# Norms one group ahead and a free bank: one change in two phases of a fused two-layer decoder

## The chip, the cores and the metric

The kernel runs on one core of one Trainium2 chip. It is one program that holds a whole two-layer decoder for 16 sequences of 128 tokens with 256 features, written by hand with explicit semaphores. The metric is the device time of the execution in microseconds (us), lower is better. Below, TensorE is the matmul engine (PE in the profile), VectorE is DVE, ScalarE is ACT, GpSimd is POOL and SyncE is SP.

## What is computed

Six blocks follow each other on a residual stream `x` of shape (16, 128, 256); each reads a layer norm of `x`:

```
x = x + attention0(layernorm(x))
x = x + retention(layernorm(x), ctx)        <- the change is here
x = x + spline_ffn(layernorm(x))
x = x + window_attention(layernorm(x))
x = x + cross_attention(layernorm(x), ctx)
x = x + moe(layernorm(x))                   <- and at the start of this one
```

Retention, with two heads of 128, `Wh` per head, and a sum over the batch inside the scores:

```
Q, K, V = xn @ Wh, ctx @ Wh, ctx @ Wh            (per head)
A       = max(|sum_batch(Q K^T / sqrt(128) * decay)|, 1)
O       = A @ V
Y       = (O - mean(O)) / sqrt(var(O) + 0.001) * gn_gamma + gn_beta
W       = relu(xn @ wg_w)
out     = (W * Y) @ wo_w
```

The last block, a mixture of 16 experts with 8 chosen per token and one shared expert:

```
shared  = ((x @ sw1.T) * relu(x @ swg.T)^2) @ sw2.T
xl      = x @ Wdown.T                                  (64 features)
p       = sigmoid(x @ Wg.T), top 8 of p + biases, scaled to a sum of 2.5
out     = shared + (sum_e p_e * expert_e(xl)) @ Wup.T
```

## The kernel before

Each block is a phase with its own queues, one list of instructions per engine, written in `phase_retention` (L717 to L1059) and `phase_moe` (L2127 to L2544). All order is that of the code; an instruction that waits on a semaphore holds up everything behind it on its engine. The eight PSUM banks are `bank[0]` to `bank[7]`. Float32 products that need precision are made by `matmul3` (L31 to L37), three products of a rounded part (`hi`) and a rest (`lo`); ScalarE writes `hi`, and VectorE the difference `lo`.

**Retention, first half.** The 16 sequences are four groups (`GROUP = 4`, `NG = 4`). For group g, VectorE's `normalise(g)` (L858) writes the four normalised sequences to `xn`, which has room for one group. TensorE's `transpose_x(g)` (L973) transposes them into `XB` (banks 0 and 1, one per half of the features). ScalarE's `round_xT(g)` (L813) and VectorE's `split_xT(g)` (L880) make `xT_hi` and `xT_lo` of it, each in one instruction of 1024 columns. TensorE's order for a group is `project_T(g)`, `transpose_x(g + 1)`, `project_gate(2g)`, `score(g)`, `project_gate(2g + 1)` (L1043 to L1049). `project_gate(p)` makes the gate of a pair of sequences in one of two banks (`GATE`), and VectorE's `take_gate(p)` (L888) turns it into `gain` and `shift`. VectorE's loop (L931 to L951) runs `normalise(g + 1)`, `take_gate(2g)`, `split_xT(g + 1)`, in group 0 then `add_out_bias()` (bias and statistics of the last four sequences, whose attention output comes late), `take_gate(2g + 1)`, and in group 0 `finish_stats` and `split_w(1)`. The norm of group 3 needs those statistics and a `pow` on GpSimd (L800).

**Retention, second half.** `mix(p)` (L1009) makes the retention output of a pair of sequences, eight pairs in all, ScalarE copies it to `O`, VectorE takes its statistics in two parts, the first four sequences (`FIRST2`) and the other twelve (`REST2`), each followed by seven small steps (`finish_stats`) and a `pow` on GpSimd (L803). Then `scale(p)` (L899) normalises and gates pair p into `xn`, in slots 0 and 1 for every pair, and so waits for the transposes of the pair before. TensorE does `transpose_wy(p)` (L1015) and then `project_out(p - 1)` (L1024); VectorE's loop (L961 to L969) is `scale(p + 1)`, `split_wyT(p)`, `restat(p - 1)`. SyncE loads the weights of all later phases in this phase (L794).

**Last phase, its start.** `project_latent(g)` (L2457) writes the latent projection of group g to `LAT_BANKS[g % 3]` (banks 2, 3, 4), `mix_latent(g)` (L2357) on VectorE makes `XL` from it. VectorE works these in between the steps of the expert choice (L2393 to L2413). `up_shared(s)` (L2461) makes the gate product of shared step s in `UG` (banks 0 and 1) and the up product in `U1[s % 3]` (banks 2, 3, 4); bank 2 is that of latent groups 0 and 3. `gate_hidden(s)` (L2361) multiplies them. Banks 6, 7 and 5 (`Y`) take the experts' down products, much later. Behind shared step 2, TensorE transposes the chosen gates (L2528 to L2531).

Of the kernel before, what the change touches and what calls it, by code (L numbers as in the profile page):

```python
# [6 lines left out]
F32 = mybir.dt.float32  # L7
F32R = mybir.dt.float32r
BF16 = mybir.dt.bfloat16
ACT = mybir.ActivationFunctionType  # L10
AX = mybir.AxisListType

B, S, D = 16, 128, 256
# [10 lines left out]
def wait(eng, sem, value):  # L24

    if isinstance(value, int) and value <= 0:
        return
    eng.wait_ge(sem, value)
# [688 lines left out]
def phase_retention(nc, a, sem, sb_, bank, X, ident, mean, var_eps, rstd, minus_half, stats, ln_tmp, banks, ret_in, out_bias, ret_loaded, ahead, ahead_loaded, kept, free_attn0, V):  # L717

    local = ExitStack()
    with local:  # L720
# [34 lines left out]
        xT_hi_ready = sem("ret_xT_hi_ready")  # L755
        xT_lo_ready = sem("ret_xT_lo_ready")
        T_done = sem("ret_T_done")
        TT_ready = sem("ret_TT_ready")
# [30 lines left out]
        with nc.Block() as block:  # L789
# [19 lines left out]
            def _(act):  # L809
# [3 lines left out]
                def round_xT(g):  # L813
                    act.wait_ge(x_transposed, g + 1)
                    wait(act, gate_made, 2 * (g - 1))
                    nc.scalar.activation(xT_hi[:, g % 2], XB, ACT.Copy).then_inc(xT_hi_ready, 1)

# [37 lines left out]
            def _(dve):  # L855
# [24 lines left out]
                def split_xT(g):  # L880
                    dve.wait_ge(xT_hi_ready, g + 1)
                    TT_(xT_lo[:, g % 2], XB, xT_hi[:, g % 2].bitcast(F32), ALU.subtract).then_inc(xT_lo_ready, 1)

# [15 lines left out]
                def scale(p):  # L899
                    dve.wait_ge(rstd2_ready, 1 if 2 * p + 1 < GROUP else 2)  # L900
                    wait(dve, wy_transposed, p)
                    for b in (2 * p, 2 * p + 1):
                        STT(O[:, b, :], O[:, b, :], mean[:, b:b + 1], gain[:, b, :], ALU.subtract, ALU.mult).then_inc(scaled, 1)
                    for b in (2 * p, 2 * p + 1):
                        dve.wait_ge(scaled, b + 1)
                        STT(xn[:, b % 2, :], O[:, b, :], rstd[:, b:b + 1], shift[:, b, :], ALU.mult, ALU.add).then_inc(wy_ready, 1)

# [21 lines left out]
                split_w(0)  # L929
                dve.wait_ge(gn_loaded, 32)  # L930
                for g in range(NG):  # L931
                    if g + 1 < NG:
                        normalise(g + 1)
                    take_gate(2 * g)
                    if g + 1 < NG:
                        split_xT(g + 1)
                    if g == 0:
                        add_out_bias()
# [16 lines left out]
                n = finish_stats(nc, dve, stat2, GROUP, stats[:, FIRST2, :], mean[:, FIRST2], var_eps[:, FIRST2], ln_tmp[:, :, FIRST2], 1e-3)  # L955
                group_stats(REST2)
                dve.wait_ge(stat2, n + B - GROUP)
                n = finish_stats(nc, dve, stat2, n + B - GROUP, stats[:, REST2, :], mean[:, REST2], var_eps[:, REST2], ln_tmp[:, :, REST2], 1e-3)
                scale(0)
                dve.wait_ge(stat2, n)  # L960
                for p in range(PAIRS + 1):  # L961
                    if p + 1 < PAIRS:
                        scale(p + 1)
                    if p < PAIRS:
                        split_wyT(p)
                    if p > 0:
                        restat(p - 1)
                    if p == EARLY // 2:
                        next_norms()  # L969

            @block.tensor
            def _(pe):
# [8 lines left out]
                def project_T(g):  # L981
                    pe.wait_ge(xT_lo_ready, g + 1)
                    wait(pe, TT_ready, g)
                    for h in range(H_):
                        ins = matmul3(nc, TB[:, h, :], (G_hi[:, h, :], G_lo[:, h, :]), (xT_hi[:, g % 2, h, :], xT_lo[:, g % 2, h, :]), first=True, last=True)
                    ins.then_inc(T_done, 1)
# [28 lines left out]
                def transpose_wy(p):  # L1015
                    pe.wait_ge(wy_ready, 2 * p + 2)
                    wait(pe, wyT_lo_ready, p - 1)
                    for k in range(KD):
                        for j in range(2):
                            at = (2 * k + j) * 128  # L1020
                            ins = nc.tensor.transpose(WYB[p % 2][:, at:at + 128], xn[:, j, k * 128:(k + 1) * 128], ident[:])
                    ins.then_inc(wy_transposed, 1)
# [1104 lines left out]
def phase_moe(nc, a, sem, sb_, bank, X, ident, mean, var_eps, rstd, minus_half, stats, ln_tmp, w, out, spare):  # L2127

    local = ExitStack()
    with local:  # L2130
# [80 lines left out]

        UG, U1, Y = bank[0:2], bank[2:5], (bank[6], bank[7], bank[5])
        XT_BANKS, LOGITS, LAT_BANKS = (bank[6:8], bank[0:2]), bank[5], bank[2:5]
        LAST_ORDER = (0, 2, 1, 3, 4, 6, 5, 7)
# [3 lines left out]
        with nc.Block() as block:  # L2218
# [105 lines left out]
            def _(dve):  # L2324
# [36 lines left out]
                def gate_hidden(s):  # L2361
# [4 lines left out]
                    else:  # L2366
                        wait(dve, downs_done, (s - NG - 6) // 2 + 1)
                        dst = hidden[:, s % 6, :]
                    TT(dst, U1[s % 3], squared[:, s % 2, :], ALU.mult).then_inc(hidden_done, 1)  # L2369

# [60 lines left out]
            def _(pe):  # L2431
# [29 lines left out]
                def up_shared(s):  # L2461
                    wait(pe, relu_done, s - 1)
                    project(UG[s % 2], 2, s).then_inc(gate_ups_done, 1)
                    wait(pe, XL_ready, (4, 2, 3, 0)[s])
                    wait(pe, hidden_done, s - 2)
                    project(U1[s % 3], 1, s).then_inc(ups_done, 1)

# [200 lines left out]
```

## Time and profile before

| | us |
|---|---|
| three runs | 1082.79, 1083.32, 1086.08 (median 1083.32) |
| the profiled execution, its own time | 1082.19 |
| its span | 1080.4 |
| TensorE busy | 1006.8 (93% of the span) |
| VectorE busy | 779.2 (72%) |
| ScalarE busy | 710.5 (66%) |
| GpSimd busy | 303.5 (28%) |

Retention runs from about 541 to 625 us of the span, the last phase from 927 us to the end. The mean granted clock of TensorE over the span is 0.968 of its full 2.4 GHz. The page's line of DMA traffic, 40 slices of 27 us, has 142 GB/s in the slice from 540 to 567 us (the weights of the later phases) and 1 to 2 GB/s in the twelve after it. In a timeline, each row has the start in us from the span's start, the time in us, the engine, the source line and operation, what is written and read, and in brackets the idle time before it and what ended it. `x8` says that eight like instructions are merged in the row.

### The profile page before, as it was taken

The page shows a single profiled execution, that of the slowest core. Times are in us where ns is not written, and L with a number is a line of the kernel's source. Part 1 is how long each engine was busy: PE and PEld are TensorE (multiplying, and loading weights), DVE is VectorE, ACT ScalarE, POOL GpSimd, SP SyncE. Part 2 cuts the span into 40 slices and gives each one's busy share as a digit, 9 for nine tenths or more (in the row PEclk, how much of TensorE's full clock was granted, in tenths as well). Part 3 has the DMA queues.
Part 4 walks back from the last instruction along what each step waited for, and adds up shares of the span by engine and source line. Part 5 has one row for each costly group of instructions (what it writes and reads, how often), then busy time and mean ns, then how long its engine had stood idle before and what let it go on. Part 6 is the DMA issues. An engine that isn't in the chain of part 4 may idle for free. (4 is left out here: it accounts for less than half of the span.)

```text
span 1080.4 us, 19089 instructions
## 1 busy us (share of the span) xinstructions
PE 1006.8 (93%) x6751; PEld 836.2 (77%) x6751; DVE 779.2 (72%) x1540; ACT 710.5 (66%) x1960; POOL 303.5 (28%) x250
## 2 busy tenths in 40 slices
PE   7999999999999999999978877899998799789998
PEld 3888889889889889888967656677776699565555
DVE  5888867667676677766667788899887344567775
ACT  5888776777777876776722356678787244448882
POOL 1343323323323333233200020244444000102442
PEclk9999999999999999999989888899999799899999
DMA  7221000000000010001050000000000000025432
GB/s 214 81 69 49 2 1 2 1 1 1 1 1 2 1 35 1 1 2 55 24 142 1 1 1 1 1 2 2 2 2 2 2 1 2 15 52 129 103 98 79
DMA packets 31837, 31.79 MB, mean 29 GB/s; under 512 B 8192, under 2 KB 23296, under 8 KB 31744
## 3 DMA queue, kind: packets, MB, share of 16 engines
q1 hardware_dynamic: 31744, 30.59, 10.3%
q8 instruction: 54, 0.88, 0.3%
q14 instruction: 39, 0.32, 0.1%
HBM read 28.35 MB, written 2.23 MB: 28 GB/s over the span
## 5 line engine op out<-in xcount | busy, mean ns | idle before, releaser
L345 POOL TENSOR_TENSOR roped_q<-roped_q,sin_q 128x512 f32<-128x512 f32 x64 | 82.0, 1281 | 301.2 <-DVE sin_q L490 301.2
L1604 ACT ACTIVATE win_P<-banks,win_neg_max 128x128 f32<-128x128 f32 x256 | 91.3, 379 | 27.4 <-DVE win_neg_max L1678 26.9
L345 POOL TENSOR_TENSOR roped_k<-roped_k,sin_k 128x512 f32<-128x512 f32 x64 | 83.3, 1301 | 46.0 <-DVE sin_k L490 46.0
L399 ACT ACTIVATE P<-banks,neg_max 128x128 f32<-128x128 f32 x256 | 90.5, 372 | 5.9 <-DVE neg_max L515 5.6
L433 ACT ACTIVATE oT_hi<-banks,bv_col 128x512 fp32r<-128x512 f32 x64 | 44.1, 689 | 74.2 <-PE banks L663 74.2
L1560 POOL TENSOR_TENSOR win_P<-win_P,win_inv 128x512 f32<-128x512 f32 x64 | 66.9, 1046 | 72.9 <-DVE win_inv L1683 72.9
L408 ACT ACTIVATE sin_k<-banks 64x512 f32<-64x512 f32 x128 | 76.0, 594 | 11.0 <-PE banks L37 9.5
L518 DVE SCALAR_TENSOR_TENSOR oT_lo<-banks,bv_col,oT_hi 128x512 fp32r<-128x512 f32 x64 | 47.9, 749 | 42.5 <-ACT oT_hi L433 42.0
L408 ACT ACTIVATE sin_q<-banks 64x512 f32<-64x512 f32 x128 | 76.0, 594 | 2.9 <-PE banks L37 0.7
L625 PE MATMUL banks<-WO_lo,oT_hi 128*128 128x256 f32 x256 | 72.9, 285 | 0.0
L625 PE MATMUL banks<-WO_hi,oT_hi 128*128 128x256 f32 x256 | 71.6, 280 | 0.0
L625 PE MATMUL banks<-WO_hi,oT_lo 128*128 128x256 f32 x256 | 71.5, 279 | 0.0
L489 DVE SCALAR_TENSOR_TENSOR roped_k<-banks,qk_bias,cos 128x512 f32<-128x512 f32 x64 | 48.0, 750 | 32.6 <-ACT sin_k L408 32.6
L638 PEld LDWEIGHTS banks<-roped_k,roped_q 128*128 128x128 f32 x512 | 67.2, 192 | 2.4
L663 PE MATMUL banks<-PT,V 128*128 128x128 f32 x512 | 68.3, 276 | 0.4 <-ACT PT L420 0.4
L638 PE MATMUL banks<-roped_k,roped_q 128*128 128x128 f32 x512 | 67.5, 275 | 0.0
L2260 POOL TENSOR_TENSOR ret_V<-ret_V 128x512 f32<-128x512 f32 x30 | 38.7, 1292 | 98.9 <-DVE ret_V L2383 98.9
L663 PEld LDWEIGHTS banks<-PT,V 128*128 128x128 f32 x512 | 62.3, 192 | 1.0 <-ACT PT L420 0.9
L2369 DVE TENSOR_TENSOR moe_hidden<-banks,moe_squared 128x512 f32<-128x512 f32 x64 | 44.1, 689 | 25.6 <-PE banks L2477 20.3
L420 ACT ACTIVATE PT<-banks 128x512 f32<-128x512 f32 x64 | 38.2, 598 | 35.4 <-PE banks L615 34.5
L489 DVE SCALAR_TENSOR_TENSOR roped_q<-banks,qk_bias,cos 128x512 f32<-128x512 f32 x64 | 48.0, 750 | 16.3 <-ACT sin_q L408 16.1
L2284 ACT ACTIVATE moe_relu<-banks 128x512 f32<-128x512 f32 x68 | 40.1, 590 | 25.5 <-PE banks L2477 15.7
(403 smaller groups left out, 3218.4 us busy)
## 6 DMA issues: line engine op xcount, KB each, us to landing
moe_gate_of<-moe_gate_rows SPq DMA_DIRECT2D x32, 256.0 KB, 4.0
X<-in_x SPq DMA_DIRECT2D x4, 512.0 KB, 6.8
stage<-in_wqT SPq DMA_DIRECT2D x4, 512.0 KB, 3.9
stage<-in_wvT SPq DMA_DIRECT2D x4, 512.0 KB, 5.9
stage<-in_woT SPq DMA_DIRECT2D x4, 512.0 KB, 4.6
ctx<-in_ctxT SPq DMA_DIRECT2D x4, 512.0 KB, 5.7
out<-X SPq DMA_DIRECT2D x8, 256.0 KB, 2.4
stage<-in_wkT SPq DMA_DIRECT2D x3, 512.0 KB, 3.8
```

The source lines that it names most:

```text
L345: nc.gpsimd.tensor_tensor(roped[w][:, p, :], roped[w][:, p, :], sin_part[w][:], ALU.add).then_inc(roped_sum[w], 1)
L399: ins = nc.scalar.activation(P[:, i, :], SC[:, i * 128:(i + 1) * 128], ACT.Exp, bias=neg_max[:, r % 2, i:i + 1], accum_out=exp_sum[:, r % ...
L408: ins = nc.scalar.activation(sin_part[w][64 * half:64 * half + 64, :], QK[w][64 * (1 - half):64 * (2 - half), :], ACT.Copy)
L433: nc.scalar.activation(flat(oT_hi[:]), PO[:], ACT.Identity, bias=bv_col[:, (r - 2) % HEADS0:(r - 2) % HEADS0 + 1]).then_inc(oT_hi_ready, 1)
L489: nc.vector.scalar_tensor_tensor(per_batch(roped[w][:, p, :]), per_batch(QK[w][:]), qk_bias[:, w, r:r + 1], table(cos), ALU.add, ALU.mult) ...
L518: nc.vector.scalar_tensor_tensor(flat(oT_lo[:]), PO[:], bv_col[:, (r - 3) % HEADS0:(r - 3) % HEADS0 + 1], flat(oT_hi[:]).bitcast(F32), ALU ...
L625: ins = nc.tensor.matmul(OUT[i // 2][:, i % 2 * D:(i % 2 + 1) * D], lhs[:, i, :], rhs[:, ur, :], start=ur == 0 and i % 2 == 0 and lhs is o ...
L638: ins = nc.tensor.matmul(SC[:, i * 128:(i + 1) * 128], roped[0][:, p, toks], roped[1][:, p, toks], start=False, stop=True, skip_group_chec ...
L663: ins = nc.tensor.matmul(PO[:, i * 128:(i + 1) * 128], V[:, ur // 4 % 2, i, h * 128:(h + 1) * 128], PT[:, i, :], start=True, stop=True)
L1560: nc.gpsimd.tensor_tensor(some, some, inv[:, h % 2, 4 * s:4 * s + 4].rearrange("p (h n) -> p h n", n=1).broadcast_to([128, 4, 128]), ALU.m ...
L1604: ins = nc.scalar.activation(P[:, h % 2, s, i, :], SC[2 * (h % 2) + s][:, i * 128:(i + 1) * 128], ACT.Exp, bias=neg_max[:, h % 2, at:at + ...
L2369: TT(dst, U1[s % 3], squared[:, s % 2, :], ALU.mult).then_inc(hidden_done, 1)
```

## The change

Retention gets the following:

- The first group is rounded and split in two halves of 512 columns, with semaphores of their own, and TensorE's first head starts after the first half.
- In VectorE's loop the norm stands one group further ahead and later in the order: `normalise(1)` before the loop, then `take_gate(2g)`, `split_xT(g + 1)`, `normalise(g + 2)`.
- `scale(0)` stands between the statistics of sequences 4 to 7 and those of 8 to 15. `scale(1)` and `split_wyT(0)` follow the finished late statistics.
- `scale(p)` writes sequence b to slot `b % 4` of `xn`, so two pairs have places, and waits for the transposes of two pairs before.

In the last phase, the up product of shared step 0 goes to bank 7 and waits for no `XL`; step 3, which uses bank 2, waits for the fourth.

```diff
@@ -754,6 +754,8 @@
         x_transposed = sem("ret_x_transposed")
         xT_hi_ready = sem("ret_xT_hi_ready")
         xT_lo_ready = sem("ret_xT_lo_ready")
+        first_hi_ready = sem("ret_first_hi_ready")
+        first_lo_ready = sem("ret_first_lo_ready")
         T_done = sem("ret_T_done")
         TT_ready = sem("ret_TT_ready")
         gate_made = sem("ret_gate_made")
@@ -813,7 +815,11 @@
                 def round_xT(g):
                     act.wait_ge(x_transposed, g + 1)
                     wait(act, gate_made, 2 * (g - 1))
-                    nc.scalar.activation(xT_hi[:, g % 2], XB, ACT.Copy).then_inc(xT_hi_ready, 1)
+                    if g == 0:
+                        nc.scalar.activation(xT_hi[:, 0, 0], XB[:, 0], ACT.Copy).then_inc(first_hi_ready, 1)
+                        nc.scalar.activation(xT_hi[:, 0, 1], XB[:, 1], ACT.Copy).then_inc(xT_hi_ready, 1)
+                    else:
+                        nc.scalar.activation(xT_hi[:, g % 2], XB, ACT.Copy).then_inc(xT_hi_ready, 1)
 
                 def take_T(g):
                     act.wait_ge(T_done, g + 1)
@@ -878,8 +884,14 @@
                         nc.vector.bn_stats(stats[:, b, :], X[:, b, :]).then_inc(stat, 1)
 
                 def split_xT(g):
-                    dve.wait_ge(xT_hi_ready, g + 1)
-                    TT_(xT_lo[:, g % 2], XB, xT_hi[:, g % 2].bitcast(F32), ALU.subtract).then_inc(xT_lo_ready, 1)
+                    if g == 0:
+                        dve.wait_ge(first_hi_ready, 1)
+                        TT_(xT_lo[:, 0, 0], XB[:, 0], xT_hi[:, 0, 0].bitcast(F32), ALU.subtract).then_inc(first_lo_ready, 1)
+                        dve.wait_ge(xT_hi_ready, 1)
+                        TT_(xT_lo[:, 0, 1], XB[:, 1], xT_hi[:, 0, 1].bitcast(F32), ALU.subtract).then_inc(xT_lo_ready, 1)
+                    else:
+                        dve.wait_ge(xT_hi_ready, g + 1)
+                        TT_(xT_lo[:, g % 2], XB, xT_hi[:, g % 2].bitcast(F32), ALU.subtract).then_inc(xT_lo_ready, 1)
 
                 def split_w(i):
                     dve.wait_ge(w_rounded, i + 1)
@@ -898,12 +910,12 @@
 
                 def scale(p):
                     dve.wait_ge(rstd2_ready, 1 if 2 * p + 1 < GROUP else 2)
-                    wait(dve, wy_transposed, p)
+                    wait(dve, wy_transposed, p - 1)
                     for b in (2 * p, 2 * p + 1):
                         STT(O[:, b, :], O[:, b, :], mean[:, b:b + 1], gain[:, b, :], ALU.subtract, ALU.mult).then_inc(scaled, 1)
                     for b in (2 * p, 2 * p + 1):
                         dve.wait_ge(scaled, b + 1)
-                        STT(xn[:, b % 2, :], O[:, b, :], rstd[:, b:b + 1], shift[:, b, :], ALU.mult, ALU.add).then_inc(wy_ready, 1)
+                        STT(xn[:, b % GROUP, :], O[:, b, :], rstd[:, b:b + 1], shift[:, b, :], ALU.mult, ALU.add).then_inc(wy_ready, 1)
 
                 def split_wyT(p):
                     dve.wait_ge(wyT_hi_ready, p + 1)
@@ -928,12 +940,13 @@
                 split_xT(0)
                 split_w(0)
                 dve.wait_ge(gn_loaded, 32)
+                normalise(1)
                 for g in range(NG):
-                    if g + 1 < NG:
-                        normalise(g + 1)
                     take_gate(2 * g)
                     if g + 1 < NG:
                         split_xT(g + 1)
+                    if g + 2 < NG:
+                        normalise(g + 2)
                     if g == 0:
                         add_out_bias()
                     if g == NG - 1:
@@ -953,18 +966,21 @@
                 group_stats(FIRST2)
                 dve.wait_ge(stat2, GROUP)
                 n = finish_stats(nc, dve, stat2, GROUP, stats[:, FIRST2, :], mean[:, FIRST2], var_eps[:, FIRST2], ln_tmp[:, :, FIRST2], 1e-3)
-                group_stats(REST2)
+                group_stats(slice(GROUP, 2 * GROUP))
+                dve.wait_ge(stat2, GROUP + 7)
+                scale(0)
+                group_stats(slice(2 * GROUP, B))
                 dve.wait_ge(stat2, n + B - GROUP)
                 n = finish_stats(nc, dve, stat2, n + B - GROUP, stats[:, REST2, :], mean[:, REST2], var_eps[:, REST2], ln_tmp[:, :, REST2], 1e-3)
-                scale(0)
+                scale(1)
+                split_wyT(0)
                 dve.wait_ge(stat2, n)
-                for p in range(PAIRS + 1):
+                for p in range(1, PAIRS + 1):
                     if p + 1 < PAIRS:
                         scale(p + 1)
                     if p < PAIRS:
                         split_wyT(p)
-                    if p > 0:
-                        restat(p - 1)
+                    restat(p - 1)
                     if p == EARLY // 2:
                         next_norms()
 
@@ -979,9 +995,11 @@
                     ins.then_inc(x_transposed, 1)
 
                 def project_T(g):
-                    pe.wait_ge(xT_lo_ready, g + 1)
+                    pe.wait_ge(*((first_lo_ready, 1) if g == 0 else (xT_lo_ready, g + 1)))
                     wait(pe, TT_ready, g)
                     for h in range(H_):
+                        if g == 0 and h == 1:
+                            pe.wait_ge(xT_lo_ready, 1)
                         ins = matmul3(nc, TB[:, h, :], (G_hi[:, h, :], G_lo[:, h, :]), (xT_hi[:, g % 2, h, :], xT_lo[:, g % 2, h, :]), first=True, last=True)
                     ins.then_inc(T_done, 1)
 
@@ -1018,7 +1036,7 @@
                     for k in range(KD):
                         for j in range(2):
                             at = (2 * k + j) * 128
-                            ins = nc.tensor.transpose(WYB[p % 2][:, at:at + 128], xn[:, j, k * 128:(k + 1) * 128], ident[:])
+                            ins = nc.tensor.transpose(WYB[p % 2][:, at:at + 128], xn[:, (2 * p + j) % GROUP, k * 128:(k + 1) * 128], ident[:])
                     ins.then_inc(wy_transposed, 1)
 
                 def project_out(p):
@@ -2210,6 +2228,7 @@
         stored = sem("moe_stored")
 
         UG, U1, Y = bank[0:2], bank[2:5], (bank[6], bank[7], bank[5])
+        up_bank = lambda s: Y[1] if s == 0 else U1[s % 3]
         XT_BANKS, LOGITS, LAT_BANKS = (bank[6:8], bank[0:2]), bank[5], bank[2:5]
         LAST_ORDER = (0, 2, 1, 3, 4, 6, 5, 7)
         ROUTER = slice(3 * EW, 3 * EW + E_)
@@ -2366,7 +2385,7 @@
                     else:
                         wait(dve, downs_done, (s - NG - 6) // 2 + 1)
                         dst = hidden[:, s % 6, :]
-                    TT(dst, U1[s % 3], squared[:, s % 2, :], ALU.mult).then_inc(hidden_done, 1)
+                    TT(dst, up_bank(s), squared[:, s % 2, :], ALU.mult).then_inc(hidden_done, 1)
 
                 def split_expert(e):
                     dve.wait_ge(we_rounded, e + 1)
@@ -2461,9 +2480,9 @@
                 def up_shared(s):
                     wait(pe, relu_done, s - 1)
                     project(UG[s % 2], 2, s).then_inc(gate_ups_done, 1)
-                    wait(pe, XL_ready, (4, 2, 3, 0)[s])
+                    wait(pe, XL_ready, (0, 2, 3, 4)[s])
                     wait(pe, hidden_done, s - 2)
-                    project(U1[s % 3], 1, s).then_inc(ups_done, 1)
+                    project(up_bank(s), 1, s).then_inc(ups_done, 1)
 
                 def up_expert(s):
                     e, g = EXPERT(s)
```

## Rows read from the trace of the kernel before

**Rows 1.** Waits of TensorE, whole span: us in total, times, longest us

```profile
PE banks L1021 <- DVE ret_xn L906: 6.9, 5, 4.2
PE banks L978 <- DVE ret_xn L864: 6.5, 3, 4.5
...
PE banks L35 <- DVE moe_XL L2359: 3.9, 1, 3.9
```

**Rows 2.** Stretch, length, busy us of PE, PEld, DVE, ACT, POOL; granted clock, DMA, GB/s

```profile
561.40:571.40 10.00, 8.71 (x55) 8.11 (x55) 5.00 (x9) 2.05 (x2) 0.00 (x0) 0.83 0.01 2
571.40:583.00 11.60, 11.60 (x94) 11.29 (x94) 6.14 (x10) 2.06 (x2) 0.00 (x0) 1.00 0.01 1
```

**Rows 3.** Timeline of ScalarE and VectorE, retention, groups 0 to 2

```profile
544.21 1.02 ACT L816 ACTIVATE ret_xT_hi<-banks 128x1024 fp32r<-128x1024 f32 x1 [1.44 <-PE banks L978]
...
545.27 1.22 DVE L882 TENSOR_TENSOR ret_xT_lo<-banks,ret_xT_hi 128x1024 fp32r<-128x1024 f32 x1 [0.71 <-ACT ret_xT_hi L816]
...
552.30 0.69 DVE L891 SCALAR_TENSOR_TENSOR ret_gain<-banks,ret_gn 128x512 f32<-128x512 f32 x1 [3.92 <-PE banks L37]
...
559.95 1.37 DVE L864 TENSOR_SCALAR ret_xn<-X,mean,rstd 128x256 f32<-128x256 f32 x4
...
565.53 0.69 DVE L891 SCALAR_TENSOR_TENSOR ret_gain<-banks,ret_gn 128x512 f32<-128x512 f32 x1 [4.20 <-PE banks L37]
...
566.73 1.22 DVE L882 TENSOR_TENSOR ret_xT_lo<-banks,ret_xT_hi 128x1024 fp32r<-128x1024 f32 x1
```

**Rows 4.** Timeline of TensorE, retention, groups 1 to 3

```profile
548.44 1.97 PE L978 MATMUL banks<-ident,ret_xn 128*128 128x128 f32 x8
...
556.48 0.39 PE L37 MATMUL banks<-ret_xT_hi,ret_G_hi 128*128 128x512 f32 x1
...
561.38 1.90 PE L978 MATMUL banks<-ident,ret_xn 128*128 128x128 f32 x8 [4.52 <-DVE ret_xn L864]
...
571.38 1.09 PE L978 MATMUL banks<-ident,ret_xn 128*128 128x128 f32 x8 [1.29 <-DVE ret_xn L864]
...
578.34 0.28 PE L35 MATMUL banks<-ret_w_lo,ret_xT_hi 128*128 128x256 f32 x1
```

**Rows 5.** Timeline of VectorE, GpSimd, TensorE, ScalarE, second half of retention

```profile
587.37 4.26 DVE L897 BATCH_NORM_STATS2 stats<-ctx_out 128x6 f32<-128x256 f32 x12
...
587.54 1.01 POOL L803 TENSOR_TENSOR rstd<-var_eps,minus_half 128x4 f32<-128x4 f32 x1 [26.50 <-DVE var_eps L61]
...
592.62 0.88 DVE L903 SCALAR_TENSOR_TENSOR ctx_out<-ctx_out,mean,ret_gain 128x256 f32<-128x256 f32 x2
...
592.78 2.44 POOL L803 TENSOR_TENSOR rstd<-var_eps,minus_half 128x12 f32<-128x12 f32 x1 [4.24 <-DVE var_eps L61]
...
593.40 0.88 DVE L906 SCALAR_TENSOR_TENSOR ret_xn<-ctx_out,rstd,ret_shift 128x256 f32<-128x256 f32 x2
...
594.43 1.09 PE L1021 MATMUL banks<-ident,ret_xn 128*128 128x128 f32 x4 [4.23 <-DVE ret_xn L906]
...
595.55 0.60 ACT L830 ACTIVATE ret_xT_hi<-banks 128x512 fp32r<-128x512 f32 x1 [4.72 <-PE banks L1021]
...
597.38 1.12 PE L1021 MATMUL banks<-ident,ret_xn 128*128 128x128 f32 x4 [1.86 <-DVE ret_xn L906]
```

**Rows 6.** Timeline of TensorE and VectorE, start of the last phase

```profile
950.34 0.40 PE L37 MATMUL banks<-moe_XT_hi,moe_w_hi 128*128 128x512 f32 x1
...
955.37 0.42 DVE L2408 TENSOR_REDUCE moe_gate_sum<-moe_gates 128x16 f32<-128x256 f32 x1
...
957.32 0.46 PE L35 MATMUL banks<-moe_XT_lo,moe_w_hi 128*128 128x512 f32 x1
...
957.62 0.69 DVE L2369 TENSOR_TENSOR moe_shared<-banks,moe_squared 128x512 f32<-128x512 f32 x1 [1.83 <-PE banks L37]
...
958.71 0.61 DVE L2412 TENSOR_TENSOR moe_gates_by_expert<-moe_gates,moe_gate_sum 128x256 f32<-128x256 f32 x1
...
962.89 0.38 PE L2530 MATMUL banks<-ident,moe_gates_by_expert 128*128 128x128 f32 x2
```

## The prediction, on record before the result

> **What bounds the kernel now.** The reading went from the page's busy shares (TensorE is busy 93% of the span, the next engine 72%) to the waits of TensorE, since with such a share only its own idle time and its clock can be won. The list of waits [rows 1] names three places in the two phases that the change touches: 6.9 us of waiting for the scaled pairs (L906), 6.5 us for the normalised groups of retention (L864), 3.9 us for `moe_XL` in the last phase. The chain that ended last reaches back only to 927.9 us, so for retention I went by the stretches and the timeline. The stretches [rows 2] show a second price: after its longest wait TensorE is granted 0.83 in the mean (part of the stretch at the lower level, 1.2 GHz), and 1.00 (2.4 GHz) in the next, which begins behind a wait of 1.29 us only. The timelines [rows 3 to 6] give the order of the work. Retention is a strict alternation in front of each group: VectorE normalises, TensorE transposes. In group 2 VectorE reaches the norm only at 559.95, behind bias, statistics and a weight split, and TensorE, done with the projection of group 1 at 556.48 + 0.23 = 556.71, stands until 561.38.
>
> All sums are against the profiled execution, 1082.19 us with a span of 1080.4; the median of the three runs is 1083.32, 1.1 above it.
>
> **Part 1, the first group in halves.** ScalarE's rounding of 1024 columns takes 1.02 [rows 3], one of 512 columns 0.60 [rows 5]. So VectorE can begin its first half at 544.21 + 0.60 + 0.04 = 544.85 and not at 545.27, 0.42 sooner. Two halves cost VectorE a little more than the whole: a 512-column one lasts 0.69 [rows 6], of which about 0.09 lies under the next instruction, so 0.60 + 0.60 against 1.22 less the same 0.09, 0.07 more. VectorE's queue from there to the norm of group 1 is unbroken (TensorE's transposes start behind it at 548.44 [rows 4]), so TensorE gets its first product of the group 0.95 sooner (545.54 against 546.49), but then waits a microsecond for that norm, and the gain that stays is 0.42 - 0.07 = 0.35 us. The two added semaphore waits have nothing behind them that is due.
>
> **Part 2, the norm one group ahead.** From here on VectorE's order is gate, split, norm, (bias, statistics, gate, a weight split). Everything is shifted by 0.35.
> - Norm of group 2: it follows the split of group 1 at 551.95 + 1.20 + 1.13 = 554.3 and ends at 555.6. TensorE is at its transposes at 556.71 - 0.35 = 556.36 and needn't wait. Before: 561.38. Gain so far 5.02 (0.35 + 4.67).
> - The cycle of one group (transposes, gate, score, gate, projection) takes 578.34 - 571.38 = 6.96 at full clock [rows 4]. The cycle from 561.38 to 571.38 took 10.00. So 3.04 are lost there: a last wait (1.45 from start to start, 1.29 as idle) and 1.59 of lower clock, which shows in the eight transposes, 1.90 against 1.09.
> - What is late next: VectorE. The norm now stands ahead of bias and statistics, and the split of group 2 is behind them all. VectorE took 559.95 - 552.30 = 7.65 from the first gate to where the norm was [rows 3]; all of that work is kept. From 552.30 - 0.35 = 551.95 add 7.65, the norm's 1.29 (1.37 less a tail of 0.08), the next gate pair's 566.73 - 565.53 = 1.20 and the split's 1.22: 563.31, and 0.15 until TensorE has it (as from 593.40 + 0.88 to 594.43 [rows 5]), 563.46. TensorE is there 6.96 less the projection after 556.36. A 512-column product takes (962.89 - 957.32)/24 = 0.232 [rows 6], six take 1.39, so it arrives at 561.93. **New wait: 1.53 us** for `ret_xT_lo` of group 2.
> - Group 3's transposes then start at 563.46 + 1.39 = 564.85, since its norm (563.22 + 1.37 = 564.59) is ready; and the `pow` on GpSimd that it needs starts at about 560.3, behind the small steps, and ends before 562.8 even at the 2.44 that twelve columns take [rows 5], where this one has four. Before: 571.38. **Gain to here 6.53 us.** From there to the first mix TensorE ran unbroken before, and does after; the 6.53 stay. The gate of pair 1, pushed behind norm, bias and statistics, comes 1.6 ahead of the weight split's end (small steps 0.99, split 0.60 [rows 5, 6]), so by 559.3; TensorE asks for its bank one gate (twelve 256-column products, 1.4) ahead of 561.93, at 560.5: about 1 us of cover, and past it each microsecond costs one.
> SP's queue of weight loads is untouched, and the page's DMA line is quiet from 567 on. GpSimd's three `pow` steps keep their order.
>
> **Part 3, the first pair ahead of the late statistics.** VectorE begins the twelve late statistics at 587.37 and takes 4.26/12 = 0.355 each [rows 5]. After four of them (588.79) comes scale(0); GpSimd has the first `rstd` at 587.54 + 1.01 = 588.55, so nothing waits. A pair takes 2 x (593.40 - 592.62) = 1.56. TensorE's first transposes come at about 590.6 and not at 594.43, but nothing can follow them but pair 1. VectorE does eight statistics (2.84) to 593.19, the seven small steps (592.62 - 591.63 = 0.99) to 594.18, scale(1) to 595.84 with its tail, TensorE at 595.99 and not at 597.38 [rows 5]. **Gain 1.39.** The same number from the other side: the two transposes stood 2.95 apart with a scale of 1.56 between them, and the 1.39 more was VectorE waiting for pair 0 to be transposed, which the second place in `ret_xn` removes. The late `rstd` comes 1.57 later than before (to 596.8) and scale(2) with it by 598.5; TensorE, with four transposes (1.1) and twelve 256-column products of pair 0 to do at the lower clock (about the 0.232 of 512 columns at the full one, 2.8), isn't at pair 2 before 599.9. In the steady state the second place gives nothing: the pairs after these are held by ScalarE's write of X, the statistics of X and the scale, in an order that stays.
>
> **Part 4, the free bank.** TensorE finished the first shared gate at 950.34 + 0.23 = 950.57 and then stood 3.86 for the fourth `moe_XL`. With bank 7 it goes on: five products of six matmuls (up 0, gate 1, up 1, gate 2, up 2) at 6 x 0.232 = 1.39 each, to 957.53. There it wants the gates. VectorE ends its reduction at 955.37 + 0.42 = 955.79; the first hidden product, which used to be late, follows at once, and from its start to the end of `moe_gates_by_expert` it is 958.71 + 0.61 - 957.62 = 1.70: 957.53, with 0.15 to TensorE 957.68. Before: 962.89. **Gain 5.21**: 3.86 of wait, about 1.3 to 1.4 of lower clock behind it. The last shared step now asks for the fourth `moe_XL`, which VectorE writes ahead of the reduction at 955.37, at about 959, so the new wait is free. The gates' way to the first weighing is shifted by the same amount.
>
> **The sum.** 6.53 + 1.39 + 5.21 = 13.13. 1082.19 - 13.13 = 1069.1, and against the median 1083.32 - 13.13 = 1070.2; I say 1070.0.
>
> **Clock, the unknown size.** No row shows what 1.53 us of waiting do. The nearest, 1.29, cost nothing (clock 1.00 behind it); 4.52 cost 1.59. I take 0, the nearer row, and keep 1.6 as the upper end. On the other side the first cycle (548.44 to 556.71 = 8.27) has 1.31 of lower clock, as its transposes show (1.97): with the shorter waits ahead of it, it can go. And pair 1 (four transposes in 1.12) will run at the lower level again; being unbroken it may return sooner, 0 to 1.0 us. The page on TensorE of the Trainium skill (TensorE: Matmul & The Clock Gate, Part 1: The HAM clock gate) says that half rate is the default which activity releases, and that one kernel shows different numbers of slow matmuls from run to run. By that rule the slow stretches may move even where the work doesn't, and the sum could be 1.6 higher or 2.3 lower by the rows above.
>
> **Rivals.**
> - The lower clock follows the new wait: 1070.0 + 1.6 = 1071.6. For it: any lengthening over the harmless 1.29. Chance 0.16.
> - The early slow stretch goes and VectorE's chain starts sooner with it: about 1068.5. Chance 0.13.
> - Only a part arrives: the gates or pair 0 chains are longer than I have them, or the phase behind retention starts by something else and swallows its 7.9: 1083.3 - 5.2 = 1078. Against it: what ends retention is TensorE's last matmul, and its loads are done by 567. Chance 0.06.
> - Slower than before: TensorE now works in shorter bursts with a wait in each, and stays at 1.2 GHz in the whole loop and the pairs. Each microsecond of work that had the full clock costs one more; it decides from 13.2 such microseconds on, which is more than the 11.6 us stretch at 1.00 [rows 2], and would give 1084 to 1090. Against it: that stretch itself, behind a wait of 1.29, and only one wait in the loop is left. Chance 0.03. The Trainium skill (TensorE: Matmul & The Clock Gate, Part 1) is on its side in so far as it calls half rate the default; the 1.00 measured here is against it.
> The forecast has 0.62. A change under 0.3% (3.2 us) is what a measurement of this kernel can't tell from none. Faster 0.95 (the forecast, the first two rivals and nearly all of the third), same 0.02, slower 0.03. The range of eight in ten, with the clock's ends (-2.3, +1.6), a microsecond of run to run and some of the third rival: 1066.5 to 1075.
>
> **What would show it.** No wait at L978 for `ret_xn` but one of about a microsecond before group 1; a wait of 1.5 at `ret_G_hi` of group 2 for `ret_xT_lo`; the loop from the first transposes to the first mix 6.5 shorter; TensorE's second pair of transposes 5.4 after the first; no L903 waiting for TensorE; the shared steps unbroken, with under 0.3 us before the gates' transposes. Wrong would be: a wait before group 2's transposes, group 2's split later than its price, or a mean clock under 0.96.

## The result, and the profile after

The changed kernel ran in 1070.03 us (median of four runs, 1066.24 to 1071.44) against 1083.05 (four runs): ratio 0.9872, 95% interval 0.9854 to 0.989. The forecast was 1070.0. The profiled execution took 1066.24 us, 15.95 less than that of before where the steps added up to 13.13, so the agreement of the medians doesn't yet show that the steps were sized right. Line numbers shift by up to 19 in the changed kernel (L978 is L994, L882 is L894, L1021 is L1039, L2530 is L2549).

TensorE's waits, whole span of the changed kernel (us in total, times, longest):

```profile
PE banks L1039 <- DVE ret_xn L918: 5.6, 5, 4.6
...
PE banks L35 <- DVE ret_xT_lo L889: 1.5, 1, 1.5
...
PE banks L994 <- DVE ret_xn L870: 1.4, 2, 0.8
...
PE banks L35 <- DVE ret_xT_lo L894: 1.3, 1, 1.3
```

The 6.5 us for the norms [rows 1] are 1.4, the 3.9 for `moe_XL` are gone from the list, and a wait of 1.3 for the split of group 2 (L894) is new. The timeline of TensorE and VectorE in the first half of retention, which answers to [rows 3, 4]:

```profile
545.59 0.47 PE L35 MATMUL banks<-ret_xT_lo,ret_G_hi 128*128 128x512 f32 x1 [1.50 <-DVE ret_xT_lo L889]
...
547.98 1.09 PE L994 MATMUL banks<-ident,ret_xn 128*128 128x128 f32 x8 [0.77 <-DVE ret_xn L870]
...
550.54 0.69 DVE L903 SCALAR_TENSOR_TENSOR ret_gain<-banks,ret_gn 128x512 f32<-128x512 f32 x1 [2.62 <-PE banks L37]
...
552.88 1.37 DVE L870 TENSOR_SCALAR ret_xn<-X,mean,rstd 128x256 f32<-128x256 f32 x4
...
554.95 1.04 PE L994 MATMUL banks<-ident,ret_xn 128*128 128x128 f32 x8
...
559.48 0.68 DVE L903 SCALAR_TENSOR_TENSOR ret_gain<-banks,ret_gn 128x512 f32<-128x512 f32 x1
...
560.68 1.22 DVE L894 TENSOR_TENSOR ret_xT_lo<-banks,ret_xT_hi 128x1024 fp32r<-128x1024 f32 x1
...
561.95 0.50 PE L35 MATMUL banks<-ret_xT_lo,ret_G_hi 128*128 128x512 f32 x1 [1.33 <-DVE ret_xT_lo L894]
...
563.44 1.03 PE L994 MATMUL banks<-ident,ret_xn 128*128 128x128 f32 x8
...
575.03 7.17 PE L1030 MATMUL banks<-ret_V,ret_AT 128*128 128x256 f32 x32
```

From the first transposes (542.99, before 543.08) to the first mix it takes 32.04 us against 39.95. The order is the predicted one: the norm of group 2 starts at 552.88, TensorE goes into its transposes at 554.95 without a wait, VectorE works from 550.54 unbroken to the end of the split at 560.68 + 1.22, and TensorE waits 1.33 for it. What isn't as predicted is the first cycle: the eight transposes at 547.98 take 1.09 us, not 1.97, and the cycle to 554.95 takes 6.97 instead of 8.27. The stretches of the same kernel (PEclk, the granted clock, is the third number from the end) say why:

```profile
core 0: us, PE busy (x) PEld busy (x) DVE busy (x) ACT busy (x) POOL busy (x), PEclk, DMA share, GB/s
541.00:549.00 8.00, 4.72 (x30) 3.46 (x29) 6.07 (x15) 3.54 (x6) 0.00 (x0) 1.00 0.28 54
549.00:560.00 11.00, 11.00 (x92) 10.69 (x91) 9.32 (x24) 2.97 (x3) 0.95 (x1) 1.00 0.98 274
560.00:575.00 15.00, 13.67 (x106) 12.85 (x104) 10.52 (x19) 2.97 (x3) 0.43 (x1) 1.00 0.13 27
583.00:592.00 9.00, 4.44 (x17) 3.30 (x16) 7.35 (x23) 1.20 (x2) 2.44 (x1) 0.62 0.00 0
```

The clock is 1.00 from 541 to 575 us, behind waits of 1.50, 0.77 and 1.33 us. It falls only behind the 4.56 us wait for pair 1 (0.62). That part of the timeline, which answers to [rows 5]:

```profile
580.68 0.86 DVE L915 SCALAR_TENSOR_TENSOR ctx_out<-ctx_out,mean,ret_gain 128x256 f32<-128x256 f32 x2
...
582.25 2.70 DVE L909 BATCH_NORM_STATS2 stats<-ctx_out 128x6 f32<-128x256 f32 x8
...
582.49 0.63 PE L1039 MATMUL banks<-ident,ret_xn 128*128 128x128 f32 x4 [0.28 <-DVE ret_xn L918]
...
585.95 0.88 DVE L915 SCALAR_TENSOR_TENSOR ctx_out<-ctx_out,mean,ret_gain 128x256 f32<-128x256 f32 x2
...
587.67 1.12 PE L1039 MATMUL banks<-ident,ret_xn 128*128 128x128 f32 x4 [4.56 <-DVE ret_xn L918]
...
588.65 0.88 DVE L915 SCALAR_TENSOR_TENSOR ctx_out<-ctx_out,mean,ret_gain 128x256 f32<-128x256 f32 x2 [0.43 <-issue]
...
592.44 0.60 PE L1039 MATMUL banks<-ident,ret_xn 128*128 128x128 f32 x4
```

Scale(0) is at 580.68 and pair 0 is transposed at 582.49, 7.46 behind the mix instead of 11.40; pair 1 comes at 587.67, 12.64 behind it instead of 14.35, a gain of 1.71 (forecast 1.39). In the last phase, answering to [rows 6]:

```profile
943.11 0.75 DVE L2378 SCALAR_TENSOR_TENSOR moe_XL<-moe_lat_hi,moe_low_rows,banks 128x512 fp32r<-128x512 f32 x1
...
945.13 0.69 DVE L2388 TENSOR_TENSOR moe_shared<-banks,moe_squared 128x512 f32<-128x512 f32 x1
...
946.23 0.62 DVE L2431 TENSOR_TENSOR moe_gates_by_expert<-moe_gates,moe_gate_sum 128x256 f32<-128x256 f32 x1
...
946.91 0.44 PE L2549 MATMUL banks<-ident,moe_gates_by_expert 128*128 128x128 f32 x2
```

The hidden product (945.13) follows the reduction at once, and the gates are transposed at 946.91. From the start of that phase's transposes to there it takes 29.22 us against 34.34 before (928.55 to 962.89).

### The profile page after: what moved, and what is told of

Same layout as the page of the kernel before. It is cut to its first block and busy times, and to the rows that moved or that the text cites. A ratio compares the mean times of both kernels' runs of the same rounds, so it can differ in the third digit from the quotient of the medians.

```text
span 1064.5 us, 19092 instructions
## 1 busy us (share of the span) xinstructions
PE 999.2 (94%) x6751; PEld 830.1 (78%) x6751; DVE 778.5 (73%) x1541; ACT 710.1 (67%) x1961; POOL 303.4 (28%) x250
## 5 line engine op out<-in xcount | busy, mean ns | idle before, releaser
L1622 ACT ACTIVATION_READ_ACCUMULATOR win_P<-banks,win_neg_max 128x1 f32 x256 | 55.8, 218 | 0.0
```

Source lines behind the costliest of these rows:

```text
L1622: ins = nc.scalar.activation(P[:, h % 2, s, i, :], SC[2 * (h % 2) + s][:, i * 128:(i + 1) * 128], ACT.Exp, bias=neg_max[:, h % 2, at:at + ...
```

## Experiments

Several of these kernels were run once. The changed kernel alone took from 1066.24 to 1071.78 us, so such a run's total says little, and what is compared is one stage in the profiles, by time and order. "The loop" is the time from retention's first transposes to the first `mix`.

**The changed kernel again.** No edit.

> The changed kernel itself, once more. The profiled execution of it gained 15.9 us where the sum of steps was 13.1, with a mean granted clock of 0.977 against 0.968 before. Theory (the waits make the gain, the slow stretches of the clock fall where they fall): the median is 13 +- 1 us under the kernel before, and a profile with a mean clock near 0.966 shows the slow stretch behind the first group of retention again, or one elsewhere, while group 2's transposes still start behind no wait and TensorE waits 1.3 to 1.6 us for the second split. Rival (the shorter waits remove the early slow stretch for good): every profile has the loop from the first transposes to the first mix at 32.0 us (as 542.99 to 575.03), and the gain is 14.5 or more.

Measured: median 1071.41 (1071.25 to 1071.78), ratio 0.9892 (0.9874 to 0.9909). The loop takes 32.06 us (545.46 to 577.52) and the transposes of group 1 again 1.09: the rival is right that the early slow stretch is gone. Its sum fails, the gain is 12 and not over 14.5, at a mean clock of 0.966. The theory's words hold: the gain is within 13 +- 1, and the slow stretches lie elsewhere. Two stretches that the change doesn't touch are longer than in the first profile: retention starts 2.47 later (545.46 against 542.99), after 40 us with a lower clock at the start of the program,

```profile
core 0: us, PE busy (x) PEld busy (x) DVE busy (x) ACT busy (x) POOL busy (x), PEclk, DMA share, GB/s
0.00:20.00 20.00, 16.29 (x43) 6.90 (x44) 10.30 (x25) 9.40 (x13) 3.23 (x8) 0.91 0.78 238
20.00:40.00 20.00, 17.37 (x82) 13.91 (x81) 13.76 (x19) 15.19 (x34) 6.79 (x6) 0.91 0.34 106
```

(1.00 in both stretches in the profile shown first), and from the spline phase's first transposes to the last phase's it takes 304.57 against 301.21.

**The parts alone: without the new bank, and with it alone.**

```diff
-                    wait(pe, XL_ready, (0, 2, 3, 4)[s])
+                    wait(pe, XL_ready, (4, 2, 3, 0)[s])
...
-                    project(up_bank(s), 1, s).then_inc(ups_done, 1)
+                    project(U1[s % 3], 1, s).then_inc(ups_done, 1)
```

and the like in `gate_hidden`, in the changed kernel; the opposite edit in the kernel before.

> The changed kernel with the last phase as it was before (shared step 0 in bank 2, waiting for the fourth XL). Theory: 5.2 us of the gain are the bank's and independent of the rest: 5.2 +- 0.3 us longer than the changed kernel in that stretch, 8 us faster than before in all (ratio 0.9925). Rival (the 3.9 us wait is only an effect of the order of the expert choice and comes back at the gates' transposes): under 2 us longer.

> The kernel before with the change of bank in the last phase alone. Theory: 5.2 us faster than before (ratio 0.9952); with the one above it adds up to the whole gain within 1 us. Rival, parts that overlap: the two don't add up to 13.

Measured: without the bank 1073.99 (1071.64 to 1078.24), ratio 0.992 (0.9892 to 0.9947); the bank alone 1078.73 (1076.26 to 1080.56), ratio 0.9954 (0.9936 to 0.9971). 1 - 0.992 and 1 - 0.9954 add up to 1.26%, the whole change measured 1.28 and 1.08%, which is within these intervals. In microseconds it isn't the sum to within 1 that was expected: 9.4 and 4.7 make 14.1, the whole brought 12.0 in the runs beside them. The stages are sharper: that from the last phase's first transposes to those of the gates takes 34.35 without the bank and 28.96 with it alone, whatever retention does. TensorE without it:

```profile
944.05 0.80 PE L35 MATMUL banks<-moe_XT_lo,moe_w_hi 128*128 128x512 f32 x1 [3.86 <-DVE moe_XL L2377]
...
952.34 0.38 PE L2548 MATMUL banks<-ident,moe_gates_by_expert 128*128 128x128 f32 x2
```

The old wait of 3.86 us is back, with a first product of 0.80 behind it; the last one ahead of the wait in [rows 6] takes 0.40 (at 950.34).

**The first group in one piece.**

```diff
-                    if g == 0:
-                        nc.scalar.activation(xT_hi[:, 0, 0], XB[:, 0], ACT.Copy).then_inc(first_hi_ready, 1)
-                        nc.scalar.activation(xT_hi[:, 0, 1], XB[:, 1], ACT.Copy).then_inc(xT_hi_ready, 1)
-                    else:
-                        nc.scalar.activation(xT_hi[:, g % 2], XB, ACT.Copy).then_inc(xT_hi_ready, 1)
+                    nc.scalar.activation(xT_hi[:, g % 2], XB, ACT.Copy).then_inc(xT_hi_ready, 1)
```

and in the same way in `split_xT` and `project_T`.

> The changed kernel with the first group rounded and split in one piece as before. Theory (the halves only bring VectorE's queue forward): TensorE's second group of transposes starts 0.35 us later than in the changed kernel (6.83 +- 0.1 us after the memset instead of 6.41), no more, although its first product comes 0.95 later. Rival (the halves matter through the clock): the wait of 2.46 us for the whole split is back and the transposes of the second group take 1.9 us instead of 1.09, so the loop is 1.3 us longer beside the 0.35.

Measured: 1070.07 in the one run. TensorE:

```profile
546.84 0.47 PE L35 MATMUL banks<-ret_xT_lo,ret_G_hi 128*128 128x512 f32 x1 [2.46 <-DVE ret_xT_lo L884]
...
548.76 1.91 PE L984 MATMUL banks<-ident,ret_xn 128*128 128x128 f32 x8
...
556.82 1.03 PE L984 MATMUL banks<-ident,ret_xn 128*128 128x128 f32 x8
```

The second transposes start 5.48 us behind the first (543.28), against 4.99: 0.49 more, not far from the 0.35. But they take 1.91, and the cycle to 556.82 takes 8.06 instead of 6.97, at a granted clock of 0.83 from 547 to 557 us. The loop is 33.63 against 32.04, 1.6 longer. The rival is right: the halves matter mostly through the clock. In all ten profiles of kernels with the halves (the changed one twice and eight variants) the transposes of group 1 take 1.09; in the three without (before, the bank alone, this one) 1.97, 1.62 and 1.91. The granted clock from 547 to 557 us is 1.00 in the ten and 0.83 to 0.85 in the three.

**One place for the scaled pairs, and pair 0 scaled late.**

```diff
-                    wait(dve, wy_transposed, p - 1)
+                    wait(dve, wy_transposed, p)
...
-                        STT(xn[:, b % GROUP, :], O[:, b, :], rstd[:, b:b + 1], shift[:, b, :], ALU.mult, ALU.add).then_inc(wy_ready, 1)
+                        STT(xn[:, b % 2, :], O[:, b, :], rstd[:, b:b + 1], shift[:, b, :], ALU.mult, ALU.add).then_inc(wy_ready, 1)
```

and `transpose_wy` reads slots 0 and 1 again; in the other kernel:

```diff
-                group_stats(slice(GROUP, 2 * GROUP))
-                dve.wait_ge(stat2, GROUP + 7)
-                scale(0)
-                group_stats(slice(2 * GROUP, B))
+                group_stats(REST2)
...
+                scale(0)
                 scale(1)
```

> The changed kernel with one place for the scaled pairs, as before (slots 0 and 1, a wait for the transposes of the pair before); the first pair is still scaled ahead of the late statistics. Theory now (the prediction gave the 1.39 us to the second place; but with pair 0 transposed 5 us earlier nothing waits for it any more): pair 1's transposes start 12.6 +- 0.1 us after the first mix, as in the changed kernel. Rival, the prediction's own words (the second place removes the wait): 14.0 or more, as before's 14.35. Either way the pairs after that stay 2.84 and 3.16 us apart in turn.

> The changed kernel with two places but the first pair scaled behind all statistics, as before. Theory (either part is enough for the 1.39): pair 1's transposes start 12.95 +- 0.1 us after the first mix, 0.3 behind the changed kernel, since the statistics of the last pair wait for ScalarE's copy by 0.2 us when no scale stands between them; pair 0's come at 11.4. Rival (scaling ahead is what counts): 14.3, as before.

Measured, one run each: 1068.49 and 1071.46. With one place, TensorE and VectorE:

```profile
589.62 1.11 PE L1039 MATMUL banks<-ident,ret_xn 128*128 128x128 f32 x4 [4.56 <-DVE ret_xn L918]
...
590.87 0.88 DVE L915 SCALAR_TENSOR_TENSOR ctx_out<-ctx_out,mean,ret_gain 128x256 f32<-128x256 f32 x2 [0.70 <-PE banks L1039]
```

Pair 1 is 12.65 behind the mix (576.97), as with two places; scale(2) now waits 0.70 for its transposes and TensorE doesn't notice (pair 2 at 594.45, 4.83 behind, against 4.77). With pair 0 late but two places, TensorE:

```profile
588.76 1.08 PE L1037 MATMUL banks<-ident,ret_xn 128*128 128x128 f32 x4 [4.22 <-DVE ret_xn L918]
...
590.25 1.11 PE L1037 MATMUL banks<-ident,ret_xn 128*128 128x128 f32 x4 [0.41 <-DVE ret_xn L918]
...
594.57 0.60 PE L1037 MATMUL banks<-ident,ret_xn 128*128 128x128 f32 x4
```

Pair 1 is 12.88 behind the mix (577.37). So either part alone brings 1.47 to 1.70 us (14.35 before), and the two together no more than the larger. The prediction gave the gain to the second place; in the kernel as changed the early scale is enough, and the second place adds nothing. The pairs after that come 3.2 and 2.84 apart in turn in both.

**The norms late, as before.**

```diff
-                normalise(1)
                 for g in range(NG):
+                    if g + 1 < NG:
+                        normalise(g + 1)
                     take_gate(2 * g)
                     if g + 1 < NG:
                         split_xT(g + 1)
-                    if g + 2 < NG:
-                        normalise(g + 2)
```

> The changed kernel with VectorE's order in the loop as before (the norm of the next group ahead of the gate). Theory: TensorE waits 4.5 us for the norm of group 2 and 1.3 for that of group 3 again, the cycle from group 2's transposes to group 3's is 10.0 against 8.49, and the loop is 4.67 + 1.45 + 1.59 - 1.33 = 6.4 us longer than in the changed kernel (38.4 from the first transposes to the first mix against 32.05). Rival (the clock behind the 4.5 us wait recovers sooner now that the early slow stretch is gone): under 5.5 longer.

Measured: 1075.87 in the one run; TensorE:

```profile
548.07 1.09 PE L993 MATMUL banks<-ident,ret_xn 128*128 128x128 f32 x8 [0.77 <-DVE ret_xn L870]
...
559.72 1.30 PE L993 MATMUL banks<-ident,ret_xn 128*128 128x128 f32 x8 [4.52 <-DVE ret_xn L870]
...
569.67 1.10 PE L993 MATMUL banks<-ident,ret_xn 128*128 128x128 f32 x8 [1.29 <-DVE ret_xn L870]
```

The waits of 4.52 and 1.29 are back and the loop takes 38.24, 6.20 longer than in the changed kernel; 6.4 was expected. The cycle from group 2 to group 3 is 9.95 (10.00 before).

**VectorE's order further on.**

```diff
                 for g in range(NG):
-                    take_gate(2 * g)
+                    if g != 1:
+                        take_gate(2 * g)
                     if g + 1 < NG:
                         split_xT(g + 1)
                     if g + 2 < NG:
                         normalise(g + 2)
+                    if g == 1:
+                        take_gate(2 * g)
...
+                        dve.wait_ge(stat, n)
+                    if g == 2:
                         split_w(1)
-                        dve.wait_ge(stat, n)
```

> The changed kernel with two further moves in VectorE's loop: the split of the output weight goes from group 0 to group 2 (0.60 us), and in group 1 the first gate pair (1.20 us) goes behind the split and the norm. Theory (the 1.32 us wait for the second split is VectorE's queue and nothing else): the wait goes, group 3's norm then ends about as TensorE is ready for it, and GpSimd's pow (ready some 1.6 us behind the small steps) is the next limit: the loop is 1.1 us shorter, 30.9 to 31.1 against 32.05. Rival (another input of that projection is late, ScalarE's T or the rounding): the wait stays over 0.8.

Measured: 1066.59 in the one run. No wait is left between group 2's and group 3's transposes, which are 6.91 apart; the loop takes 30.64, 1.40 shorter (1.1 was expected, 30.9 to 31.1). The theory is right that the wait was VectorE's queue; GpSimd's `pow` isn't a limit yet:

```profile
554.87 1.03 PE L998 MATMUL banks<-ident,ret_xn 128*128 128x128 f32 x8
...
561.78 1.03 PE L998 MATMUL banks<-ident,ret_xn 128*128 128x128 f32 x8
```

**The new wait made longer.**

```diff
                     take_gate(2 * g)
+                    if g == 1:
+                        for i in range(2):
+                            TT_(flat(pair(O, i)), flat(w_in[:, 1]), flat(w_hi[:, 1]).bitcast(F32), ALU.subtract).then_inc(delayed, 1)
```

`delayed` is a semaphore that nothing waits for.

> The changed kernel with two more subtractions of 512 columns (results unused, written to the place of O before it is needed) on VectorE ahead of the split of group 2, 1.20 us, so that TensorE's new wait grows from 1.32 to 2.5 us. Theory (a wait of 2.5 us is enough to bring the lower clock, as the 2.46 us did in the first group before the change, but the 1.32 isn't): the loop grows by 1.2 + 0.5 to 1.6, the stretch behind the wait has a mean granted clock under 0.95. Rival (only the 4.5 us waits bring it): 1.2 and no more, clock 1.00. This shows how near to the edge the changed kernel is.

Measured: 1072.43 in the one run. The loop takes 34.87 (542.98 to 577.85), 2.83 longer for 1.20 us of work. TensorE behind the wait, and the stretches:

```profile
563.15 0.50 PE L35 MATMUL banks<-ret_xT_lo,ret_G_hi 128*128 128x512 f32 x1 [2.53 <-DVE ret_xT_lo L895]
...
565.37 1.91 PE L998 MATMUL banks<-ident,ret_xn 128*128 128x128 f32 x8
```

```profile
core 0: us, PE busy (x) PEld busy (x) DVE busy (x) ACT busy (x) POOL busy (x), PEclk, DMA share, GB/s
554.00:562.00 8.00, 6.63 (x53) 6.17 (x51) 7.86 (x22) 1.94 (x2) 1.38 (x1) 1.00 1.02 242
562.00:575.00 13.00, 11.85 (x76) 11.01 (x77) 7.50 (x13) 3.08 (x3) 0.00 (x0) 0.87 0.00 0
```

Group 3's eight transposes take 1.91, and the clock is 0.87: of the 2.83 us, 1.20 are the added work, and the 1.6 that are left are the clock's.

**A filled wait, and both improvements.**

```diff
+                    if p == 0:
+                        pe.wait_ge(O_ready, 5)
+                        for _ in range(32):
+                            nc.tensor.matmul(MIX[0][:, 0:256], w_hi[:, 1, 0, 0:128], w_hi[:, 1, 1, :], start=True, stop=True)
```

> The changed kernel with 32 matmuls that nothing uses (128x256, of the gate weights' rounded part, into bank 0) on TensorE between the transposes of pair 0 and of pair 1, where it waits 4.56 us. Theory (the wait costs its lower clock behind it): about 3.8 of the wait are filled, pair 1's transposes still start 12.65 us after the first mix, take 0.6 instead of 1.1, and pair 2's follow 2.9 instead of 4.4 to 5.2 us later: 1.5 to 2.3 us shorter to the start of the spline phase (41.1 to 41.7 from the first mix now). Rival (the pairs are held by VectorE and ScalarE there): pair 2 as late as now, under 0.5 us.

> The changed kernel with the two further moves in VectorE's loop and with the 32 unused matmuls. Theory: 1.4 us (measured for the moves) + 1.5 to 2.3 (the filled wait), so about 3.3 us under the changed kernel, 1067.5 to 1068.5 in the median, ratio to before 0.986. Rival (chance of the clock elsewhere covers it): 1070 or more.

Measured: with the filled wait 1065.91 in the one run; both together 1064.94 (five runs, 1063.46 to 1068.05), ratio to before 0.9834 (0.9807 to 0.9861), the fastest version here and 2.6 us under the lower end of its forecast (1067.5 to 1068.5). TensorE with the filled wait:

```profile
587.97 0.66 PE L1039 MATMUL banks<-ident,ret_xn 128*128 128x128 f32 x4 [0.73 <-DVE ret_xn L918]
...
590.75 0.60 PE L1039 MATMUL banks<-ident,ret_xn 128*128 128x128 f32 x4
```

Pair 1 starts 12.66 behind the mix as expected, its transposes take 0.66, and pair 2 is 2.78 behind, not 4.77. From the first mix to the spline phase it takes 39.47 against 41.45 and 41.08 in the changed kernel's two profiles: 1.6 to 2.0 us for work that nobody reads. In both together that stage takes 39.47 again and the loop 30.65. The median is 5 to 6.5 us under the changed kernel's; the two stages account for 3.0 to 3.4 of it. The rest isn't theirs; in the profiles it lies in stretches that neither edit touches (below, at the sum).

## Why the prediction was right, step by step

The time and the direction were right, the list of removed waits too; two of the four sizes were off, and the closeness of the total is luck.

- **Norms ahead.** Right. Both old waits and the slow stretch behind the longer one went; the new wait stands where VectorE's queue put it, 1.33 of idle; the cycle with it takes 8.49 against 6.97 without, so 1.52 in all for a forecast of 1.53. It left the clock alone. Undone alone, this part is worth 6.20 us; by the prediction's terms 4.67 + 1.45 + 1.59 - 1.53 = 6.18.
- **Halves.** Mis-sized: 0.35 was forecast as what VectorE's queue gains, 1.6 is what it measured (33.63 against 32.04). The term that was wrong is the clock in the first cycle: the prediction left its 1.31 in the sum and gave its going away, as a rival, a chance of 0.13. It comes with the edit: the one wait of 2.46 becomes two of 1.50 and 0.77, and in none of the ten profiles does the clock fall behind these.
- **Pair 0 ahead, two places.** The size was 1.71 for 1.39. Of the 0.32 more, 0.23 are the twelve late statistics: 4.28 us from start to start in one piece, before and with the late pair, and 1.31 + 2.74 in two, where ScalarE's last copy is done long before. The step that failed is the sentence that the second place removes the wait. It would, alone; beside the early scale it does nothing. Behind pair 1 the clock's share varies: from the first mix to the spline phase the two profiles with the old retention take 43.52 and 42.62, the nine with the new one and no filled wait 41.08 to 42.13, so the whole second half gained between 0.5 and 2.4.
- **Free bank.** Right: 5.12 and 5.31 in the two profiles, 5.39 as the difference of the two part experiments, for 5.21.
- **The sum.** Retention, from its first transposes to the spline phase's, went from 83.47 us to 73.49 and 73.14, the last phase's start from 34.34 to 29.22 and 29.03. That is 15.1 to 15.6 us, 2 to 2.5 more than forecast. The medians are only 12 to 13 apart. What is between was found in stretches outside of the change, with a lower clock in some executions. One is the beginning: retention's first transposes come at 542.4 to 543.3 us in ten of the thirteen profiles, at 544.9 to 545.5 in three, all of the changed kernel and its variants. The other is the spline to cross phases: 301.2 to 302.7 us in eight profiles, 304.4 to 304.9 in five, one of them with the old retention; in these five the granted clock from 80 to 100 us behind the spline phase's first transposes is 0.64 to 0.66, in the other eight 0.83. So 1070.0 against 1070.03 is luck: two misses of opposite sign. Whether the changed kernel falls into these slower stretches more often than the old one, or this is chance of few profiles, stays open.
- **Rivals.** The clock behind the new wait of 1.33 us didn't fall. Behind 2.53 it does, and takes 1.6, so the rival's price was right. The slower rival, a loop at 1.2 GHz, has nothing for it: 1.00 in the whole loop.

## What to carry to other kernels

When two edits each remove the same wait, undo them one at a time before crediting either. Where TensorE waits for long, price the wait twice, once as idle time and once as the 1.2 GHz stretch behind it. Where the wait can't be removed, try to cut it in two, or to fill it with matmuls that end before it does; both paid here. After a step is moved ahead, add up the queue of the engine that moved it: here that gave the next late item to 0.01 us (1.52 for 1.53), and the next edit to 0.3 (1.40 for 1.1). And when the total agrees, compare the stages before believing the sum.

## What the runs showed of the hardware

In these two phases, waits of 1.29, 1.33 and 1.50 us left TensorE's granted clock at 1.00, and those of 2.46, 2.53, 3.86 and 4.5 us were followed by a stretch at 1.2 GHz, each costing 1.3 to 2.8 us beyond the wait (the 3.86 in the last phase the least; the most behind the 4.52 with the bank alone, where the cycle takes 11.23 us instead of 10.00). The page on TensorE of the Trainium skill (TensorE: Matmul & The Clock Gate, Part 1) says that activity releases the half rate, and the filled wait agrees. From 582 to 592 us its granted clock is 1.00, where the changed kernel has 0.62 from 583 to 592. The same part of that page of the Trainium skill says that the number of slow matmuls differs from run to run. The stretch behind a given wait did differ (pair 1 to pair 2 took from 4.42 to 5.18 us behind the same 4.56), and at the start of the cross phase the four transposes behind a wait of 2.63 us took 0.66 in one profile of the changed kernel and 1.11 or 1.12 in the other twelve profiles. In the spline phase, eight transposes behind a wait of 2.7 us took 1.06 in six profiles and 1.57 to 1.92 in seven. So what follows a wait of 2.6 to 2.7 us differed from run to run, and the 2.46 and 2.53 rest on three profiles and one.
